# Cross-attention and a top-2 mixture of experts on one core: expert outputs weighted on leaving PSUM and scattered with addition into one row per token

## The reference, cut to what matters

```python
x = x + xattn(layernorm(x), ctx, ctx, ...)       # x: 8 x 512 tokens of 256; attention within blocks of 64
x = x + ffn(layernorm(x), ...)

def ffn(x, gate_w, expert_bias, w_up, w_down):   # 8 experts, top 2, inner width 1024
    weights = softmax(x @ gate_w.T + expert_bias)
    top_w, top_i = top_k(weights, 2)
    top_w = top_w / (sum(top_w) + 1e-6)
    sparse_w = sum(one_hot(top_i, 8) * top_w)
    out = 0
    for e in range(8):
        out = out + sparse_w[e] * (gelu(x @ w_up[e].T) @ w_down[e].T)
    out = (out - mean(out)) * rsqrt(var(out) + 1e-5)   # per token
    return out + x
```

## Time and profile before

| | us |
|---|---|
| median of 3 runs | 823.22 (821.9 to 823.74) |
| the profiled execution, whole | 824.23 |
| its span from first to last instruction | 822.4 |
| PE busy | 720.0 (88% of the span) |
| DVE busy | 536.5 (65%) |
| ACT busy | 363.5 (44%) |
| POOL busy | 441.4 (54%) |
| mean granted TensorE clock | 0.932 |

### The profile page before, as it was taken

The page is one execution under the profiler, slowest core; times in us unless marked ns, Lnnn a source line. Parts: engine busy times, 40 slices in busy tenths (PEclk is TensorE's granted clock), DMA queues, the critical chain, the costliest instruction groups (busy, mean ns, idle before and its releaser), DMA issues.

```text
span 822.4 us, 20968 instructions
## 1 busy us (share of the span) xinstructions
PE 720.0 (88%) x6400; PEld 648.0 (79%) x6401; DVE 536.5 (65%) x1182; ACT 363.5 (44%) x657; POOL 441.4 (54%) x584
## 2 busy tenths in 40 slices
PE   4999999999999718599999999999999999999200
PEld 4999999999999514498899999998899898998100
DVE  4889888888888579455555555555555555554295
ACT  2877777777777403122222222222222222222184
POOL 3777787788787407524444444344443444422287
PEclk9999999999999855699999999999999999999655
DMA  4333333333332100111111111111111111110594
GB/s 157 109 108 121 104 121 103 120 104 119 103 121 85 41 7 0 54 38 53 53 51 47 44 49 45 45 51 51 51 51 45 45 51 45 45 38 27 171 304 164
DMA packets 39875, 64.54 MB, mean 78 GB/s; under 512 B 5408, under 2 KB 30240, under 8 KB 39840
## 3 DMA queue, kind: packets, MB, share of 16 engines
q1 hardware_dynamic: 31632, 42.37, 16.0%
q0 software_dynamic: 7488, 20.46, 7.7%
q10 hardware_dynamic: 720, 1.26, 0.5%
HBM read 45.46 MB, written 18.61 MB: 78 GB/s over the span
## 4 chain that ended last, share of the span: by engine, by line
PE 87%; DVE 4%; issue 3%; DMA 2%; POOL 2%; ACT 1%; SPq 0%; ACTq 0%; DVEq 0%; POOLq 0%
PE ps_a L530 25%; PE ps_b L544 25%; PE ps_b L433 7%; PE ps_a L391 4%; PE ps_b L400 4%; PE ps_c L412 4%; PE ps_c L417 3%; PE ps_a L468 3%; PE ps_a L455 2%; PE ps_c L498 2%; PE ps_c L514 2%; PE ps_a L479 1%; PE ps_c L378 1%; PE ps_a L443 1%; DMA w_hi<-y_rows 1%
## 5 line engine op out<-in xcount | busy, mean ns | idle before, releaser
L530 PE MATMUL ps_a<-area,w_hi 128*128 128x256 f16 x1248 | 207.7, 274 | 1.7 <-DVE area L795 1.7
L544 PE MATMUL ps_b<-w_hi,area 128*128 x1248 | 206.4, 273 | 0.0
L1055 POOL DMA_INDIRECT y_rows<-area x78 | 77.9, 999 | 209.4 <-ACT area L940 197.5
L530 PE MATMUL ps_a<-area,w_lo 128*128 128x256 f16 x624 | 170.7, 274 | 0.0
L544 PE MATMUL ps_b<-w_lo,area 128*128 x624 | 170.1, 273 | 0.0
L935 ACT ACTIVATE area<-ps_a 128x512 f32<-128x512 f32 x156 | 93.1, 597 | 142.0 <-PE ps_a L530 142.0
L530 PEld LDWEIGHTS ps_a<-area,w_hi 128*128 x1248 | 122.3, 98 | 16.1 <-issue 2.1
L544 PEld LDWEIGHTS ps_b<-w_hi,area 128*128 128x128 f16 x1248 | 122.1, 98 | 14.1
L793 DVE TENSOR_SCALAR area<-ps_c 128x512 f16<-128x512 f32 x39 | 27.0, 691 | 151.7 <-PE ps_c L514 151.7
L805 DVE SCALAR_TENSOR_TENSOR area<-area 128x512 f16<-128x512 f32 x156 | 108.3, 694 | 5.4
L940 ACT ACTIVATE area<-ps_b 128x512 f32<-128x512 f32 x39 | 23.3, 597 | 181.1 <-PE ps_b L544 181.1
(11 more groups left out here) (129 smaller groups left out, 1250.2 us busy)
## 6 DMA issues: line engine op xcount, KB each, us to landing
area<-weights SPq DMA_DIRECT2D x32, 512.0 KB, 3.3
w_hi<-y_rows SPq DMA_DIRECT2D x32, 256.0 KB, 4.0
resid<-x_in SPq DMA_DIRECT2D x32, 128.0 KB, 2.1
area<-ctx_t SPq DMA_DIRECT2D x32, 128.0 KB, 2.1
xn_rows<-area SPq DMA_DIRECT2D x32, 128.0 KB, 1.7
out<-w_lo SPq DMA_DIRECT2D x16, 256.0 KB, 2.6
area<-xn_rows,area POOLq DMA_INDIRECT x78, 2.8
y_rows<-area POOLq DMA_INDIRECT x78
```

The lines of the kernel that those rows point to most:

```text
L530: mm = pe.matmul(ps_h[:, q, (ic % 2) * SLOTS:(ic % 2 + 1) * SLOTS], w[:, bass.ds(first + (hc * I + ic * P), P)], r[b][:, hc, :], start=(n ...
L544: mm = pe.matmul(ps_y[:, b, v * D:(v + 1) * D], g[b][:, ic, v * P:(v + 1) * P], w[:, bass.ds(first + (EXPERT_COLS + ic * D), D)], start=(n ...
L1055: pool.indirect_dma_start(y_rows[:, :], bass.IndirectOffsetOnAxis(ap=didx[b][:, v:v + 1], axis=0), y_s[b][:, v * D:(v + 1) * D], None).the ...
```

## The change

The router's mixing weight is applied in the expert stage, where ACT takes the output from PSUM: each of the two 128-slot halves of a tile is copied on its own with a weight per partition. For that `mix_w` is transposed on PE, scaled on ACT, written by SP to a DRAM array `mix_rows` with one 4-byte entry per (choice, token) pair, and POOL gathers from it, for each tile one step ahead of its use, one entry per slot (an index copy and two indirect DMAs more per tile). `y_rows` holds one row per token; SP fills it with zeros during attention (four DMAs of nine row tiles each, and a small one for the padding entries of `mix_rows`), and the scatter adds in DRAM. The scatter of tile k now also waits until that of tile k-1 has landed. `slot_row` holds the row for the scatter (two more DVE instructions before `routed`). In the last stage one row per token is loaded, the weighting (ACT) and the weighted sum (DVE) are gone, POOL adds the residual of the first tile of a group and DVE that of the second.

```diff
@@ DRAM arrays
-        y_rows = nc.dram_tensor("y_rows", [TOPK * TOKENS + 2 * SLOTS, D], ...)
+        y_rows = nc.dram_tensor("y_rows", [TOKENS + 2 * SLOTS, D], ...)
+        mix_rows = nc.dram_tensor("mix_rows", [TOPK * TOKENS + 2 * SLOTS, 1], ...)
@@ last-stage tiles
-        y_in = w_hi[:, :].bitcast(F32).rearrange("p (g j n) -> p g j n", g=GROUPS, j=TOPK)
-        f_s, o_s = ...
+        y_in, o_s = (w[:, 0:2 * TILES * D].bitcast(F32)... for w in (w_hi, w_lo))
+        zeros = w_lo[:, 2 * E * EXPERT_COLS - 2 * D:2 * E * EXPERT_COLS].bitcast(F32)
@@ sync, attention step
+                if isinstance(j, int) and 2 <= 2 * j + u < 6:
+                    n = (TOKENS + 2 * SLOTS) // P // 4
+                    first = n * (2 * j + u - 2)
+                    if first == 0:
+                        sp.wait_ge(zeros_r, 1)
+                        sp.dma_start(mix_rows[TOPK * TOKENS:..., :]..., zeros[:, 0:2 * SLOTS // P]).then_inc(zero_out, 16)
+                    sp.dma_start(y_rows[first * P:(first + n) * P, :].rearrange("(a p) d -> p a d", p=P),
+                                 zeros.unsqueeze(1).to_broadcast([P, n, D])).then_inc(zero_out, 16)
@@ sync, after attention
+            sp.wait_ge(mix_t_r, 1)
+            sp.dma_start(mix_rows[0:TOPK * TOKENS, :].rearrange("(g p) d -> g (p d)", p=P), mix_t[:, :]).then_inc(mix_out, 16)
@@ sync, last stage: load and store
-                for c in range(TOPK):
-                    sp.dma_start(y_in[:, bass.ds(g, 1), c]..., y_two[bass.ds(g, 1), c]...).then_inc(yin[u], 16)
+                sp.dma_start(y_in[:, bass.ds(CG * g, CG), :], y_g[bass.ds(g, 1)]...).then_inc(yin[u], 16)
...
                     sp.wait_ge(c_out, g + 1)
+                    sp.wait_ge(c_add, g + 1)
@@ tensor
+            pe.wait_ge(mix_r, 1)
+            pe.transpose(ps_c[0:TOPK * TILES, 1, 0:P], mix_w[:, :, :].rearrange("p j t -> p (j t)"), ident).then_inc(mix_ps, 1)
@@ vector, before everything else; routing
+            dve.memset(zeros, 0.0).then_inc(zeros_r, 1)
...
-            dve.tensor_scalar(slot_token[:, :], slot_dest[:, :], TOKENS - 1, None, ALU.bitwise_and).then_inc(routed, 1)
+            link(dve.tensor_scalar(slot_token[:, :], slot_dest[:, :], TOKENS - 1, None, ALU.bitwise_and))
+            link(dve.tensor_scalar(pair_f, dest_f, float(TOKENS), -float(TOKENS), ALU.is_ge, ALU.mult))
+            dve.tensor_tensor(slot_row[:, :], dest_f, pair_f, ALU.add).then_inc(routed, 1)
@@ vector, last stage
+                at_g = g - 4
+                if group_valid(at_g):
+                    dve.wait_ge(c_ap, CG * (at_g + 1))
+                    r = bass.ds(CG * at_g + 1, 1)
+                    dve.tensor_tensor(o_s[:, r, :], o_s[:, r, :], resid[:, r, :], ALU.add).then_inc(c_add, 1)
                 at_g = g - 3
                 ... (the shift, as before)
                 if group_valid(g):
+                    dve.wait_ge(yin[u], 16 * (j + 1))
                     for r in range(CG):
-                        dve.wait_ge(c_f0, t + 1)
-                        dve.scalar_tensor_tensor(f_s[...], y_in[..., 1, ...], mix_w[:, 1, ...], f_s[...], ALU.mult, ALU.add).then_inc(c_f1, 1)
...
-                        dve.bn_stats(c_st[u][:, r, :], f_s[...]).then_inc(c_stats, 1)
+                        dve.bn_stats(c_st[u][:, r, :], y_in[...]).then_inc(c_stats, 1)
@@ scalar
+            act.wait_ge(mix_ps, 1)
+            act.activation(mix_t[:, :], ps_c[0:TOPK * TILES, 1, 0:P], ACT.Copy, scale=1.0 / (G_SCALE * W_SCALE)).then_inc(mix_t_r, 1)
...
-                    act.activation(y_s[b], ps_y[:, b, :], ACT.Copy, scale=1.0 / (G_SCALE * W_SCALE)).then_inc(y_r, 1)
+                    act.wait_ge(wgat[b], 16 * SUBS * (half + 1))
+                    for v in range(SUBS):
+                        act.activation(y_s[b][:, v * D:(v + 1) * D], ps_y[:, b, v * D:(v + 1) * D], ACT.Copy,
+                                       scale=mix_slot[b][:, v:v + 1]).then_inc(y_r, 1)
...
-                if group_valid(g):      # the two weightings of choice 0
-                        act.activation(f_s[...], y_in[..., 0, ...], ACT.Copy, scale=mix_w[:, 0, ...]).then_inc(c_f0, 1)
@@ gpsimd, experts
                     since(pool, scat[b], 16 * SUBS * half)
-                    pool.tensor_copy(didx[b], slot_dest[...]).then_inc(didx_r, 1)
-                    pool.wait_ge(y_r, k + 1)
+                    pool.tensor_copy(didx[b][:, 0:SUBS], slot_row[...]).then_inc(didx_r, 1)
+                    pool.wait_ge(y_r, SUBS * (k + 1))
+                    if not isinstance(k, int) or k > 0:
+                        pool.wait_ge(scat[1 - b], 16 * SUBS * (half + b))
                     for v in range(SUBS):
                         pool.indirect_dma_start(y_rows[:, :], bass.IndirectOffsetOnAxis(ap=didx[b][:, v:v + 1], axis=0),
-                                                y_s[b][:, v * D:(v + 1) * D], None).then_inc(scat[b], 16)
+                                                y_s[b][:, v * D:(v + 1) * D], None, compute_op=ALU.add).then_inc(scat[b], 16)
+                k, half, b = here(j, u, 1)
+                if moe_valid(k):
+                    pool.tensor_copy(widx[b][:, 0:SUBS], slot_dest[:, bass.ds(SUBS * k, SUBS)]).then_inc(widx_r, 1)
+                    pool.wait_ge(widx_r, k + 1)
+                    for v in range(SUBS):
+                        pool.indirect_dma_start(mix_slot[b][:, v:v + 1], None, mix_rows[:, :],
+                                                bass.IndirectOffsetOnAxis(ap=widx[b][:, v:v + 1], axis=0)).then_inc(wgat[b], 16)
@@ gpsimd, last stage
-                    r = bass.ds(CG * at_g, CG)
-                    pool.wait_ge(c_ap, CG * (at_g + 1))
+                    r = bass.ds(CG * at_g, 1)
+                    pool.wait_ge(c_ap, CG * at_g + 1)
                     pool.tensor_tensor(o_s[:, r, :], o_s[:, r, :], resid[:, r, :], ALU.add).then_inc(c_out, 1)
```

More of the change, by code:

```diff
@@ L93, in program @@
         mix_w = sb("mix_w", [P, TOPK, TILES])
+        mix_t = sb("mix_t", [TOPK * TILES, P])
+        slot_row = sb("slot_row", [P, UNITS], I32)
         slot_dest = sb("slot_dest", [P, UNITS], I32)
@@ L101, in program @@
         gate_bias = cst[:, C_GATE_B:C_END]
-        AREA = 11500
+        AREA = 11312
         area = sb("area", [P, AREA])
@@ L176, in program @@
         y_s = [carve(SUBS * D) for _ in range(2)]
-        gidx, didx = ([carve(SUBS).bitcast(I32) for _ in range(2)] for _ in range(2))
+        gidx, didx, widx = ([carve(SUBS).bitcast(I32) for _ in range(2)] for _ in range(3))
+        mix_slot = [carve(SUBS) for _ in range(2)]
         CG = 2
         GROUPS = TILES // CG
-        y_in = w_hi[:, :].bitcast(F32).rearrange("p (g j n) -> p g j n", g=GROUPS, j=TOPK)
-        f_s, o_s = (w_lo[:, h * 2 * TILES * D:(h + 1) * 2 * TILES * D].bitcast(F32).rearrange("p (t n) -> p t n", t=TILES) for h in range(2))
+        y_in, o_s = (w[:, 0:2 * TILES * D].bitcast(F32).rearrange("p (t n) -> p t n", t=TILES) for w in (w_hi, w_lo))
+        zeros = w_lo[:, 2 * E * EXPERT_COLS - 2 * D:2 * E * EXPERT_COLS].bitcast(F32)
         at[0] = 0
@@ L273, in program @@
         routed = sem("routed")
+        zeros_r, zero_out = sem("zeros_r"), sem("zero_out")
+        mix_r, mix_ps, mix_t_r, mix_out = sem("mix_r"), sem("mix_ps"), sem("mix_t_r"), sem("mix_out")
+        widx_r, wgat = sem("widx_r"), [sem(f"wgat{i}") for i in range(2)]
         gat = [sem(f"gat{i}") for i in range(2)]
@@ L282, in program @@
         outs = sem("outs")
-        c_f0, c_f1, c_stats, c_mvr, c_ver, c_rsr, c_nmr, c_ap, c_out = (
-            sem(n) for n in ("c_f0", "c_f1", "c_stats", "c_mvr", "c_ver", "c_rsr", "c_nmr", "c_ap", "c_out"))
+        c_add, c_stats, c_mvr, c_ver, c_rsr, c_nmr, c_ap, c_out = (
+            sem(n) for n in ("c_add", "c_stats", "c_mvr", "c_ver", "c_rsr", "c_nmr", "c_ap", "c_out"))
         MOE_FIRST, MOE_LAST = 4, 36
@@ L332, in step @@
                     sp.dma_start(xn_rows[bass.ds(t * P, P), :], xn2).then_inc(xn2_out[b], 16)
+                if isinstance(j, int) and 2 <= 2 * j + u < 6:
[3 more added lines that the diff above has]
+                        sp.wait_ge(zeros_r, 1)
+                        sp.dma_start(mix_rows[TOPK * TOKENS:TOPK * TOKENS + 2 * SLOTS, :].rearrange("(p a) d -> p (a d)", p=P),
+                                     zeros[:, 0:2 * SLOTS // P]).then_inc(zero_out, 16)
+                    sp.dma_start(y_rows[first * P:(first + n) * P, :].rearrange("(a p) d -> p a d", p=P),
+                                 zeros.unsqueeze(1).to_broadcast([P, n, D])).then_inc(zero_out, 16)
                 if isinstance(j, int) and 2 * j + u == TILES:
@@ L343, in _ @@
             sp.wait_ge(y_ps, SLOT_TILES)
-            y_two = y_rows[0:TOPK * TOKENS, :].rearrange("(j g t p) d -> g j p t d", j=TOPK, t=CG, p=P)
-            out_g = out.rearrange("(g t) p d -> g p t d", t=CG)
+            y_g, out_g = (v.rearrange("(g t) p d -> g p t d", t=CG) for v in (y_rows[0:TOKENS, :].rearrange("(t p) d -> t p d", p=P), out))
```

(37 more changed lines are left out.)

7 lines of the change are left out of this document (4 added, 3 removed).

## The result

The changed kernel takes 857.0 us (median of 4 runs, 851.88 to 859.64) against 823.35 before: the ratio is 1.0405, 95% interval 1.0354 to 1.0455. It is slower by 4%, where 818.2 was forecast. The profiled execution is the fastest of the four, 851.88 us with a span of 850.0, so its 27.6 us over the span before is the low end of the loss.

| stage | before | after | difference | forecast |
|---|---|---|---|---|
| attention, to the first routing reduction | 290.1 | 300.6 | +10.5 | +0.5 |
| routing, to PE's first transpose | 45.7 | 46.2 | +0.5 | +0.5 |
| experts, to the end of the last copy out of PSUM | 430.4 | 452.2 | +21.8 | 0, +0.1 at the end |
| from there to the first load of the last stage | 4.5 | 8.4 | +3.9 | +1.0 |
| last stage | 51.7 | 42.6 | -9.1 | -7.1 |

A forecast was written before the change was run, and what follows sets the result against it. PE bounds the experts, and only the last stage had something to win: -7.1 us there, +2.1 added on the path, sum -5.0, so 818.2 for the median (819.2 profiled) from 823.22; forecast range 815 to 821, wider range 812 to 833.

The forecast's parts named there:

- rival A: Expert loop: POOL becomes the bound through longer adding issues; +15 us (833) at +0.5 per issue, +53 (871) at +1.0; chance 0.22.
- zero fill: Attention: the fill delays the context DMA behind it in SP's queue, just in time; +0.5 us (0 to 7).
- rival D: Attention: the zero fill costs its high end, +6.5 us, 825 in all; chance 0.05.
- POOL in the experts: Expert loop: POOL's work with the weight gather takes 10.32 of 10.92 us per tile, so it fits; +0.
- the issue looks like fixed work: Argument against POOL becoming the expert bound: row gather and scatter cost the same although directions differ.
- The last scatter: End of the experts: adding in DRAM needs a read of the destination before landing; +1.0 us (0 to 2.41).
- The last stage: Last stage: filling -4.1 us, middle groups -2.2, draining -0.8; together -7.1.
- The knot: Last stage: DVE's add waits for ACT, ACT for the shift behind an earlier add; 2.2 us per group.
- Rival B: Last stage: the DVE-ACT loop is looser, POOL's 1.8 us per group sets the pace; -4.8 more, 813.4; chance 0.18.
- rival C: Last stage: DVE and POOL adds block each other, 2.5 us per group, +4, 822, no change; chance 0.09.
- Routing +0.5: Routing: two more DVE instructions before `routed`, about 0.25 us each, while PE idles for its gather; +0.5.
- The PSUM copy: End of the experts: ACT's copy in two halves of 256 columns, hidden in the loop, counted once; +0.1 us (+0 to +0.3).

The follow-up runs named there:

- first experiment: The changed kernel with the two scatters of a tile writing without addition: 825.39 us, ratio 1.0038 to the kernel before.
- last experiment: The changed kernel with each scatter issuing only 64 of its 128 rows: 842.19 us with addition, 829.5 us without, one execution each.
- third experiment: The changed kernel with the four zero fills issued just behind the x load instead of ahead of it: 848.42 us, ratio 1.0324 to the kernel before.
- kernel with both repairs: The changed kernel with one six-index copy per tile on POOL and the zero fills issued behind the x load: 820.15 us, ratio 0.9971.
- sixth experiment: The kernel with both repairs, with DVE's last-stage shift moved ahead of its residual add: 818.71 us, ratio 0.9959 to the kernel before.

## Why the prediction was wrong

The mechanism that made the kernel slower was for the larger part rival A, with a chance of 0.22; the zero fill (rival D, 0.05) added more than its high end. Step by step:

**POOL in the experts: this step failed.** It took the adding issue at the price of the nearest row, 0.99, while the upper bound, twice that, would have decided the sign. The issue takes 1.62. The rest of the sum was near: without addition POOL fits with little to spare (first experiment). The tolerance of 0.3 us per issue was stated; the cost was twice that. Put into rival A's own formula, 0.63 gives (10.32 + 1.26 - 10.92) x 38 = 25 us; the stage lost 21.8. That agreement is partly luck, since two things that the formula leaves out nearly cancel. POOL's tile takes 11.77 on average, not 11.6, because copies and issues stretch: the 34 tiles from the first scatter on take 400.2 us, 28.9 more than in the kernel before. Then the row gathers are over, since they run three tiles ahead, and POOL makes up part of it: the last scatters follow 8.4 us apart, and 7.0 come back. "It fits, so +0" was a step of a function with a cliff 0.6 us away. The argument "the issue looks like fixed work" is true of the plain issue (0.83 of 0.99, last experiment), but it rested on gather and scatter, neither of which adds, and the addition has a fixed part of its own.

**The zero fill: the wrong victim.** The term was +0.5 with an end at +7; it cost 10.5. This step failed too. I followed the context load (needed 4.3 us after it is issued) and overlooked the `x` load, which SP issues directly behind the fill and whose statistics stand at the head of DVE's next step. I had its row in front of me and read it only as a time stamp. The fill's own length was near: 5.4 to 6.6 us from issue to landing, where I had 5.1 (42.2 to 47.3). The context, my victim, is waited for as well, 5.6 us in all in the changed kernel; but in the third experiment, where only the context stands behind the fill and is waited for 3.6 us, the stage loses 0.2.

**The last scatter: right in kind, short in size.** +1.0 for the landing is +1.2 by the rows. What was missed is the wait for the landing of tile 37, declared free below 7 us. That holds in the loop, where there are 10.9 us; behind the last tile PE runs two down products in a row, 5.24 apart, and POOL was late as well. With the longer issues that makes +3.9, and +3.1 in the kernel with both repairs.

**The last stage: right.** Filling 6.2 us (6.9 forecast), 2.01 per group (2.2 in the loop and 1.8 at the end, 2.12 on average, were forecast), draining 1.72 (1.65). In the loop it is 2.05 where 2.2 was forecast, because the two starts that I put at 0.30 and 0.2 take 0.26 and 0.16. The knot was read correctly from the order of instructions, and the sixth experiment confirms that it bound (28.7 us from shift to shift in place of 30.2). Rival B (1.8 per group) and rival C (2.5) are both out; the blocking that C spoke of exists, yet it costs only when nothing else is in the way.

**Routing +0.5: right. The PSUM copy** costs +0.24, not +0.1: two halves take 0.84.

## What to carry to other kernels

Before a new kind of instruction is put on a queue, ask how long it may be before that queue turns into the bound, and if the answer lies inside the bounds of its unknown cost, that unknown decides the forecast, not the sum around it. A large store put into an in-order queue is paid by the next small load behind it: find who uses that load first, and place the store behind the loads that are needed soonest (10.5 us against 0.2 here). Indices for several indirect DMAs belong in one table with one copy: that alone brought back 22 us of the expert stage, and with the fill moved the change wins about 0.3% (0.4% with the shift ahead of the add).

## What the runs showed of the hardware that was not expected

- An indirect DMA that adds takes POOL 1.62 us for 128 rows of 1 KB, a plain one 0.99; at 64 rows 1.45 and 0.91. A gather of 4 bytes per row takes 1.04, one of 1 KB per row 0.97 (medians).
- In the last tile, the second of two adding issues lands 3.62 us after its start, of two plain ones 2.41.
- Between two indirect issues without a copy POOL needs 0.30 us, behind a copy and its semaphore 0.82 to 1.01 in the rows shown.
- While the experts run at 11.8 us per tile the granted clock stays at full (1.00 in every stretch from 368 to 799 us), although PE has gaps: in the emptiest one it is busy for 76.8 of 82 us.
